# Linear attention with two half-weighted norms on one core: a written-out closing, another opening order, and matmuls on a weight matrix in TensorE's pauses

## What is computed

```python
x = x + 0.5 * _L0_ffn_ref(_layernorm(x), ...)
x = x + _L0_attn_ref(_layernorm(x), Wq, Wk, Wv, Wo, bo)
x = x + 0.5 * _L0_ffn_ref(_layernorm(x), ...)

# attention: 16 heads of 32, causal, linear
phi_q, phi_k = elu(x @ Wq.T) + 1, elu(x @ Wk.T) + 1
S = S + phi_k[:, None] * v[None, :]      # token by token
z = z + phi_k
out = (phi_q @ S) / (phi_q . z + 1e-5)
return out @ Wo.T + bo
```

## Time and profile before

| | |
|---|---|
| median of 3 runs | 940.27 us (939.8 to 940.8) |
| profiled execution: time | 940.58 us |
| profiled execution: span of the trace | 938.8 us |
| granted TensorE clock, mean | 0.987 |
| TensorE (matmul) busy | 898.5 us (96%), 10252 instructions |
| VectorE busy | 827.4 us (88%) |
| ScalarE busy | 758.4 us (81%) |
| GpSimd busy | 711.6 us (76%) |
| mean DMA rate | 149 GB/s |

### The profile page before, as it was taken

How to read it: one execution, slowest core, us unless ns; L and a number is a source line. 1 busy time by engine, 2 the same in 40 slices (tenths; PEclk the granted TensorE clock), 3 DMA queues, 4 the chain that set the end, 5 groups by cost and what they waited for, 6 DMA issues and landing times. The chain is left out here.

```text
span 938.8 us, 29969 instructions
## 1 busy us (share of the span) xinstructions
PE 898.5 (96%) x10252; PEld 525.8 (56%) x10252; DVE 827.4 (88%) x1531; ACT 758.4 (81%) x1327; POOL 711.6 (76%) x875
## 2 busy tenths in 40 slices
PE   3899999999999999999999999999999999999974
PEld 2455556555555655555565555556565555655542
DVE  6888899999999999999999999999999999998764
ACT  5978788888888888888888888888888888888861
POOL 2277787788777788878778987777898777779761
PEclk9999999999999999999999999999999999999986
DMA  8286887866687666768767666876766787776762
GB/s 290 41 174 123 171 159 156 138 153 151 144 179 156 149 142 148 151 148 179 156 146 144 146 151 151 179 156 141 146 149 148 154 171 161 144 121 128 128 118 68
DMA packets 421405, 139.81 MB, mean 149 GB/s; under 512 B 402544, under 2 KB 402544, under 8 KB 421360
## 3 DMA queue, kind: packets, MB, share of 16 engines
q1 hardware_dynamic: 404496, 106.73, 60.5%
q10 hardware_dynamic: 16864, 32.51, 10.6%
HBM read 21.76 MB, written 16.78 MB: 41 GB/s over the span
## 5 line engine op out<-in xcount | busy, mean ns | idle before, releaser
L1302 PE MATMUL PJ<-wT,XT 128*128 128x512 f16 x2304 | 525.1, 379 | 1.7 <-DMA XT<-XH 1.4
L1302 PEld LDWEIGHTS PJ<-wT,XT 128*128 128x128 f16 x2304 | 216.6, 98 | 245.3 <-DMA XT<-XH 3.2
L459 POOL TENSOR_TENSOR A<-AM,A 128x512 f16<-128x512 f32 x256 | 292.5, 1162 | 35.4 <-ACT A L677 35.4
L1401 PE MATMUL PJ<-wT,AT 128*128 128x512 f16 x768 | 178.6, 383 | 1.2 <-DMA AT<-ATTN 1.2
L451 POOL TENSOR_SCALAR_AFFINE_SELECT AM<-AM 128x512 f32<-128x512 f32 x128 | 82.0, 641 | 113.1 <-ACT AM L667 113.1
L677 ACT ACTIVATE A<-AM 128x512 f16<-128x512 f32 x256 | 154.0, 630 | 12.6 <-POOL AM L451 11.3
L1372 PE MATMUL AV<-SS,QS 128*128 128x33 f16 x1024 | 112.3, 178 | 4.9 <-POOL A L459 4.4
L1375 PE MATMUL AV<-VN,A 128*128 128x33 f16 x3072 | 116.9, 178 | 0.0
L1401 PEld LDWEIGHTS PJ<-wT,AT 128*128 128x128 f16 x768 | 71.6, 98 | 79.8 <-issue 2.7
L1375 PEld LDWEIGHTS AV<-VN,A 128*128 128x128 f16 x3072 | 109.3, 96 | 3.7
L992 DVE TENSOR_TENSOR AM<-SC,causal 128x512 f32<-128x512 f32 x128 | 87.5, 684 | 22.9 <-PE SC L1352 22.9
(11 more groups left out here) (101 smaller groups left out, 1531.8 us busy)
## 6 DMA issues: line engine op xcount, KB each, us to landing
out_dram<-Y ACTq DMA_DIRECT2D x32, 512.0 KB, 3.1
X<-in_L_attn_x_dram ACTq DMA_DIRECT2D x30, 512.0 KB, 3.5
X<-in_L_attn_x_dram SPq DMA_DIRECT2D x2, 512.0 KB, 8.0
A<-in_L_attn_Wk_dram SPq DMA_DIRECT2D x1, 1024.0 KB, 8.3
A<-in_L_attn_Wq_dram SPq DMA_DIRECT2D x1, 1024.0 KB, 10.5
QS<-in_L_attn_Wv_dram SPq DMA_DIRECT2D x1, 1024.0 KB, 12.7
QS<-in_L_attn_Wo_dram SPq DMA_DIRECT2D x1, 1024.0 KB, 16.0
XT<-XH SPq DMA_TRANSPOSE x64, 3.4
```

What stands on the lines that cost most here:

```text
L459: g.tensor_tensor(A[:, b, LO, hg], AM[:, k % 4], A[:, b, HI, hg], ALU.subtract).then_inc(a_lo.sem, 1)
L1302: ins = t_.matmul(PJ[b], XT[:, w, c, b * C:(b + 1) * C], wT[m_][:, m, c, :], start=(c, w, m) == todo[0], stop=(c, w, m) == todo[-1])
L1401: ins = t_.matmul(PJ[b], AT[:, b, w, c * C:(c + 1) * C], wT[3][:, m, c, :], start=(c, w, m) == todo[0], stop=(c, w, m) == todo[-1])
```

## The change

Four parts.

1. `run` stops two steps earlier for the closing (steps 28 and 29 instead of 28 to 33), and every engine gets a `closing()` with its own order for what is left: `fourth` (attention of chunk 29), `third` (30), `second` (31, the last one) and `last` (the back part of 31).
2. In the last attention step the odd groups are treated as the even ones: VectorE masks all eight (`copy_scores` and `cut` do nothing there), and VectorE also makes the low half of A for the odd groups (a new `split_a` on VectorE, with a semaphore of its own, `a_lo_last`); GpSimd keeps the even ones. The last chunk's 1/sqrt is made for each batch apart (`rstd2_of_tile`), and each batch is stored by its own DMA (`store_tile`).
3. TensorE gets `keep_busy(n)`: n matmuls of 128x512 on a block of the query weights into the bank of `project_out(0)`, whose result nobody reads: 14 behind `attend(0, ..)` and 12 behind `attend(1, ..)` of the last chunk.
4. The order of the opening is another on every engine; operations and their number stay.

```diff
-            for s in range(steps - 4, steps + 2):
+            for s in range(steps - 4, steps - 2):
                 body(Step(0, s))
...
@@ SyncE, opening @@
+                first.turn_k(0)
+                first.turn_k(1)
                 first.turn_q(0)
-                first.turn_k(0)
                 first.turn_x(0)
+                first.turn_x(1)
                 first.turn_q(1)
-                first.turn_x(1)
-                first.turn_k(1)
                 second.turn_k(0)
...
-            sp.wait_ge(y_stored.sem, y_stored.at(steps - 1))
+            sp.wait_ge(y_stored.sem, y_stored.at(steps - 1, 1))
...
@@ GpSimd @@
+                    def rstd2_of_tile(b):
+                        if b == 0 and st.has(-2):
+                            pool.wait_ge(*g2_done.upto(st.chunk(-2), 1))
+                        pool.wait_ge(*stat2_done.upto(back, b))
+                        g.tensor_scalar(var2[:, b:b + 1], stat2[:, b, 1:2], 1.0 + EPS, EPS * EPS, ALU.mult, ALU.add).then_inc(var2_done.sem, 1)
+                        pool.wait_ge(*var2_done.upto(back, b))
+                        g.tensor_tensor(rstd2[:, b:b + 1], var2[:, b:b + 1], neg_half[:, b:b + 1], ALU.pow).then_inc(rstd2_done.sem, 1)
...
+                third.spread_k(0)
+                third.spread_k(1)
+                third.spread_q(0)
+                third.cut(1, 1)
+                third.split_a(1, 0)
+                third.split_a(1, 1)
+                third.cut(1, 3)
+                third.spread_q(1)
...
+                third.split_s(0)
+                third.split_s(1)
+                third.x1_bias()
+                second.rstd2_of_x2()
+                second.split_a(1, 0)
+                second.split_a(1, 2)
+                last.rstd2_of_tile(0)
+                last.rstd2_of_tile(1)
...
@@ ScalarE @@
+                    def store_tile(b):
+                        act.wait_ge(*y_done.upto(back, b))
+                        a.dma_start(out[b, bass.ds(back * C, C), :], Y[:, b]).then_inc(y_stored.sem, 16)
...
                 square(0, 0)
-                early.next_x()
                 square(0, 1)
                 square(0, 2)
+                early.next_x()
                 square(0, 3)
...
@@ VectorE @@
+                    def split_a(b, hg):
+                        if not ATTEND or PROJECT or hg % 2 == 0:
+                            return
+                        k = b * GROUPS + hg
+                        dve.wait_ge(*a_hi.upto(s, k))
+                        v.tensor_tensor(A[:, b, LO, hg], AM[:, k % 4], A[:, b, HI, hg], ALU.subtract).then_inc(a_lo_last.sem, 1)
...
+                second.mask(1, 2)
+                second.mask(1, 3)
+                second.reciprocals(0)
+                second.back_gain(0)
+                second.back_y(0)
+                second.quotient(0)
+                second.split_a(1, 3)
+                second.back_gain(1)
+                second.attn_low(0)
+                second.back_y(1)
+                second.reciprocals(1)
+                second.quotient(1)
+                second.attn_low(1)
+                second.add_out(0)
+                second.out_stats(0)
+                second.out_mean(0)
+                second.add_out(1)
+                second.out_stats(1)
+                second.out_mean(1)
+                last.back_gain(0)
+                last.back_y(0)
+                last.back_gain(1)
+                last.back_y(1)
...
@@ TensorE @@
+                    def keep_busy(n):
+
+                        pe.wait_ge(*x2_done.upto(back, 0))
+                        for i in range(n):
+                            t_.matmul(PJ[0], wT[0][:, HI, 0, 0:P], wT[0][:, HI, 0, :], start=True, stop=True)
...
+                second.scores(0, 0)
+                second.scores(0, 1)
+                second.scores(0, 2)
+                third.attend(1, 0)
+                third.attend(1, 1)
+                second.scores(0, 3)
+                third.project_v(1)
+                second.scores(1, 0)
+                second.scores(1, 1)
+                third.update(1, 0)
+                third.update(1, 1)
+                third.project_out(0)
+                third.project_out(1)
+                second.scores(1, 2)
+                second.scores(1, 3)
+                second.attend(0, 0)
+                second.attend(0, 1)
+                second.keep_busy(14)
+                second.attend(1, 0)
+                second.attend(1, 1)
+                second.keep_busy(12)
+                second.project_out(0)
+                second.project_out(1)
```

More of the change, by code:

```diff
@@ L358, in _, with closing @@
             run(sp, body)
-            sp.wait_ge(y_stored.sem, y_stored.at(steps - 1))
+            def closing():
+                fourth, third, second = ops(Step(0, steps - 3)), ops(Step(0, steps - 2)), ops(Step(0, steps - 1))
+                fourth.turn_q(0)
+                fourth.turn_attn(0)
+                fourth.turn_attn(1)
+                fourth.turn_x(0)
+                fourth.turn_x(1)
+                fourth.turn_q(1)
+                fourth.turn_k(1)
+                third.turn_k(0)
+                third.turn_q(0)
+                third.turn_k(1)
+                third.turn_q(1)
+                third.turn_attn(0)
+                third.turn_attn(1)
+                second.turn_attn(0)
+                second.turn_attn(1)
+            closing()
+            sp.wait_ge(y_stored.sem, y_stored.at(steps - 1, 1))
         @block.gpsimd
@@ L457, in split_a @@
                         k = b * GROUPS + hg
+                        if not PROJECT and hg % 2:
+                            return
                         pool.wait_ge(*a_hi.upto(s, k))
@@ L535, in _, with closing @@
             run(pool, body)
+            def closing():
+                fourth, third, second, last = ops(Step(0, steps - 3)), ops(Step(0, steps - 2)), ops(Step(0, steps - 1)), ops(Step(0, steps))
+                fourth.cut(1, 3)
+                fourth.spread_q(0)
+                fourth.split_a(1, 1)
+                fourth.split_a(1, 2)
+                fourth.split_a(1, 3)
+                fourth.rstd1_of_x1()
+                fourth.spread_k(1)
+                third.cut(0, 1)
+                third.split_a(0, 0)
+                fourth.spread_q(1)
+                third.cut(0, 3)
+                fourth.split_s(0)
+                fourth.split_s(1)
+                third.rstd2_of_x2()
+                third.split_a(0, 1)
+                third.split_a(0, 2)
+                third.split_a(0, 3)
+                third.spread_k(0)
[6 more added lines that the diff above has]
+                third.spread_q(1)
+                third.split_a(1, 2)
+                third.split_a(1, 3)
+                second.split_a(0, 0)
+                second.split_a(0, 2)
+                third.split_s(0)
[6 more added lines that the diff above has]
+                last.rstd2_of_tile(1)
+            closing()
         @block.scalar
@@ L658, in copy_scores @@
                     def copy_scores(b, hg):
-                        if not ATTEND:
+                        if not (ATTEND and PROJECT):
                             return
```

362 lines of the change are left out of this document (276 added, 86 removed).

## The result

The changed kernel takes 932.88 us (median, 931.69 to 933.88), the kernel before, beside it, 940.79 (939.8 to 943.88): ratio 0.9912, 95% interval 0.9896 to 0.9927, so 8.3 us faster by the ratio and 7.9 by the two medians. The profiled execution took 931.69, the fastest of the six, with a span of 929.8 us and a mean granted clock of 0.996.

A forecast was written before the change was run, and what follows sets the result against it. TensorE bounds the kernel: its full loop plus standing at both ends, with half clock near the end. Closing 6.7 and opening 2.0 sum to 8.7 us, from a 940.27 median to 931.6; range 928.5 to 936.0.

The forecast's parts named there:

- The opening: Before the loop: first scores from 50.87 to about 49.3, an earlier second-chunk key projection; 2.0 us gained, ends 0 and 3.2.
- its turning starts about 1.6 us later than for 24.27: Opening: the first x's low half now stands behind three weights, delaying its transpose about 1.6 us; counted against the gain.
- It could be 2.8 earlier: Opening: the second chunk's key projection of batch 1, which waited 0.99 us for x, could come 2.8 us earlier.
- The closing: From the last key projections to the last store: 6.7 us gained, ending at 932.1 instead of 938.8.
- Standing in the last but one chunk: Closing: TensorE stands 2.1 us, 1.3 for batch 0's queries and a mask, 0.8 for turned attention; chunk ends at 908.1.
- Turned 3.1 us later: Last chunk: each batch's attention is transposed in 3.1 us, batch 0 ready at 918.7, batch 1 at 921.6.
- A gain of 3.8, of which 2.5 is the clock: Last chunk: second output projection ends at 924.2 instead of 928.03, 2.5 from full clock (5.14 against 2.6), rest earlier start.
- The tail: Behind the last projection: shorter statistics, one gain and result (1.55 instead of 3.0 us), store 0.7 us shorter; end at 932.1.
- Shared port: Rival, closing: two of VectorE's new splits each wait out a 1.16 us GpSimd split, 2.3 us, giving 933.9; chance 0.10.
- The clock falls all the same: Rival, closing: small pauses of 894 to 903 us bring TensorE to 1.2 GHz, +3 us, giving 934.6; chance 0.10.
- Four transposes one after another: Rival, closing: K and Q transposes are served singly at 5.8 us each, 13.4 us later, giving 945.0; chance 0.06.
- Fillers delay: Rival, last chunk: pauses shorter than the fillers, at most 5.6 us lost, 939.2 without opening gain, no change; chance 0.04.

The follow-up runs named there:

- e11: The changed kernel with ScalarE's load of the next x back between the first two squares of the opening: 933.66 us, ratio 0.9919.
- e3: The changed kernel without both groups of fillers (26 extra matmuls): 933.5 us, ratio 0.9921.
- e6: The changed kernel with chunk 30's 512 KB store issued behind the last chunk's first scale, and without the fillers: 933.42 us, ratio 0.9926.
- e9: The changed kernel with the last chunk's 1/sqrt made for both batches at once and both stored by one DMA: 936.6 us, ratio 0.9942.
- e4: The changed kernel with attention of chunk 30's batch 1, first half, ahead of the last chunk's third score group on TensorE: 933.41 us, ratio 0.9915.
- e2: The changed kernel with the old order of the opening on all five engines (closing alone): 937.17 us, ratio 0.9952.
- e10: The changed kernel with the first group of 14 fillers and without the second of 12: 935.05 us, ratio 0.9936.
- e1: The kernel before with the new order of the opening on all five engines (opening alone): 937.13 us, ratio 0.9962.

## Why the prediction was right, and where not

The sum was right (8.7 forecast, 8.3 measured; 931.6 against 932.88, inside the forecast's own 929.0 to 933.5), but it holds two errors that cancel, and that they do is luck.

**The opening, 2.0 forecast, 3.6 alone in its run.** That is above my upper end of 3.2, but the interval (2.3 to 4.8) takes it in. The step that failed is "its turning starts about 1.6 us later than for 24.27". The DMA was issued 1.2 us later (20.86 instead of 19.64), but the 24.27 didn't hang on it. Before, the transpose had landed at 23.0, 3.4 us after issue, and TensorE was still turning weights behind a wait for VectorE:

```profile
22.53 1.94 PE L1279 MATMUL SC<-ident,A 128*128 128x128 f32 x8 [1.13 <-DVE wT L908]
```

Now it lands at 24.0, after 3.1 us, and the projection starts at 24.14: the delay went into a slack of 1.2 us that I hadn't seen. The bound was wrong too: I took ScalarE's and VectorE's idle time to be what an order can win, but a stall of TensorE can also be a transpose queued in the wrong place, and that isn't seen in either's busy time. "It could be 2.8 earlier" pointed at the place: x of batch 1 is issued with that of batch 0 at 43.83 and not at 52.45. The 0.90 us ahead of ScalarE's second square are gone, but VectorE's list took them away and not the moved load (`e11`).

**The closing, 6.7 forecast, 4.5 alone in its run, 4.1 in the profile.** Behind T0, forecast and measured:

| | forecast | measured | 
|---|---|---|
| chunk 30's second output projection ends | 30.3 | 31.0 |
| quotient of batch 0 ready | 35.9 | 37.2 |
| first output projection starts | 40.9 | 42.3 |
| second output projection starts | 43.8 | 46.5 |
| from its end to the end of the span | 7.9 | 7.6 |

- *Standing in the last but one chunk.* "Going through the steps ... issues at 894.2" and "with landings of 5.8 to 6.1": batch 1's queries were issued 17.8 us behind T0 instead of 16.4 and took 6.5. SyncE's four issues take 1.8 to 3.1 us each and stand 0.25 us apart, for which my steps had no term. The chunk ends 0.7 later than forecast. (They stand in the order K, Q, K, Q, so K of batch 1 is third of the four and not second, as the text on the order has it.)
- *The chain to the quotient of batch 0* is 0.65 longer than mine: in it the gain waits 0.62 us for ScalarE.
- *"Turned 3.1 us later"* held for batch 0 and failed for batch 1, with 4.4 to 4.5. This is the largest error, 1.4 us, and it comes with the fillers (`e3`, `e6`), to which I had given no cost.
- *"A gain of 3.8, of which 2.5 is the clock"* failed most clearly. The second projection ends 0.9 us earlier behind T0 and not 3.8. The clock did come back (5.14 to 2.76 us for the first projection), but the second hangs on its own transpose, and my sum itself went by that (921.6). In before too, the second one waited 0.20 us for its transpose when the slow first one was done, so a faster first projection by itself would have moved it by nothing, and the label "2.5 is the clock" was wrong from the start. What the fillers were worth is 0.6 us, with intervals that overlap. The 2.9 us between 3.8 and 0.9 are the three items above (0.7, 0.65, 1.4) and 2.76 us for a projection instead of 2.6.
- *The tail* held: 2.9 forecast, 3.2 measured, 2.5 of it taken back by `e9`.
- *The fillers fit*: 3.18 and 2.75 us, together 0.3 more than forecast, with TensorE standing 1.25 and 0.55 behind them. They delay nothing on TensorE, but they come with the late transpose.

**The rivals.** *Shared port*: VectorE's four new splits, all instructions of that line in after:

```profile
L1161 DVE TENSOR_TENSOR A<-AM,A x4: 680/682/692, 896.1 to 910.0; 128x512 f16<-128x512 f32 x4
```

None is stretched by the 1.16 us of a GpSimd split; my 0.70 held. The Trainium skill (SBUF — State Buffer, "SBUF: two separate sides") would have such a pair exclude each other; of the four only the first meets a GpSimd split (896.05 and 896.52), by 0.2 us, so no run here shows the rule at work or broken; it cost nothing. *The clock falls all the same* came true in part: it fell at 892.3, behind pauses of 0.48 and 0.56 us, and cost nothing, since it filled the wait for the queries (`e4`). My "the point is a pause near 2.2 us" was false. *Four transposes one after another* (945.0) didn't come: landings were 4.5 to 6.5 us, overlapping. *Fillers delay* didn't come as I had written it.

Of what I wrote as signs, these held: both output projections at 2.76, no wait for keys, first scores before 50 us, and the last store late in the tail (it lands 2.1 us behind its issue). "A clock of 0.5 behind 894" came true, as a sign of wrong, without a loss, and with it the sign "PEclk 1.00 until the end of the second output projection" failed.

## What to carry to other kernels

A stretch at half clock is worth its excess only if nothing else is waited for behind it: look whether the next instruction's other operand (here a DMA transpose) has landed by the time that the fast version would need it. Added instructions can have a price elsewhere: with the fillers a transpose of the same size landed 1.3 us later. Ahead of filling pauses, split the serial tail by tile: one gain, one result and half a store less behind the last aggregate was 2.5 of 4.1 us. And hand-written lists of several engines are one object: TensorE's list alone, taken from the old version, cost 11 us where the whole new set gained 3.6.

## What the runs showed of the hardware

- The granted clock fell to 1.2 GHz behind two short pauses (0.48 and 0.56 us in after), and in kernels with TensorE's same order there it stayed at 1.00 behind 0.32 and 0.56 (`e2`), 0.41 and 0.56 (`e11`), and 0.52 and 0.56 (`e6`). With pauses of 1.00 and 1.36 us, further apart, it stayed at 1.00 as well (`e4`). The length of one pause doesn't tell whether it falls.
- The length of a DMA transpose depends on more than its size. One of 256 KB, the last of its kernel, landed after 3.1 us in four kernels, and after 4.4 to 4.9 in the ten in which a packet of an instruction queue (0.02 MB) fell into it. That the packet is the cause isn't shown.
- Issuing a DMA transpose kept SyncE for 1.2 to 3.1 us, one after another.
- Where a kernel ends with 256 KB stores they landed after 2.1 us; the last 512 KB ones landed after 2.8 to 3.1. The Trainium skill (DMA: Bandwidth & Descriptors, "Anatomy of one DMA — SWDGE (gpsimd) path") gives a fixed 2.0 us and bytes over 436 GB/s, measured on GpSimd's path, an estimate of 2.6 and 3.2 us for these, which go by ScalarE's queue. The trace agrees at 3.1, and the small store is half a microsecond faster than that.
- The opening isn't the same from run to run. ScalarE's first square, which reads the key weights, starts between 9.99 and 11.60 us. The first projection of 12 matmuls takes 3.22 to 4.75 us, at a recorded clock of 1.00 (0.50 in `e10` alone, with 4.43). In two executions with the new opening the second chunk's x was waited for 1.3 and 1.8 us, where in after it wasn't. So the 4.9 us in the profiled pair are above the 3.6 of `e1`, and single executions can't rank openings that differ by a microsecond.
